# Gated attention with routed experts: the preparation as one written order per engine

## Chip, cores and metric

One core of a Trainium2 chip runs the whole program. The metric is the device time in microseconds (us) from start to end, the median of several runs.

## The reference

Four batches of 1024 tokens of width 256 pass a cross-attention on 77 context rows each, and then a mixture of 8 experts of which each token uses 2. Everything is float32.

```python
def layernorm(x, g, b):
    mu = jnp.mean(x, axis=-1, keepdims=True)
    var = jnp.mean(jnp.square(x - mu), axis=-1, keepdims=True)
    return (x - mu) * jax.lax.rsqrt(var + EPS) * g + b
...
    scores = jnp.einsum('bqe,bke->bqk', q, k) * scaling
    attn = jax.nn.softmax(scores, axis=-1)
    ctx = jnp.einsum('bqk,bke->bqe', attn, v)
    return ctx @ Wo + bo
...
    gate_logits = jnp.einsum('bsd,de->bse', x, gate_w) + gate_b
    gate_weights = jax.nn.softmax(gate_logits, axis=-1)
    topk_values, topk_indices = jax.lax.top_k(gate_weights, TOP_K)
    hidden = jax.nn.relu(jnp.einsum('bsd,edh->bseh', x, w1) + b1)
    expert_out = jnp.einsum('bseh,ehd->bsed', hidden, w2) + b2
    sel = jnp.take_along_axis(expert_out, topk_indices[..., None], axis=2)
    return jnp.sum(topk_values[..., None] * sel, axis=2)
...
x = x + jnp.tanh(g_xattn[0]) * xattn(_layernorm(x), ctx_768, ...)
x = x + jnp.tanh(g_ffn[0]) * ffn(_layernorm(x), ...)
```

## The kernel before

Each engine has its own program, written out by hand, and runs it strictly in order; semaphores are the only link. After some small folding of weights (to about 38 us) comes the **preparation** (to about 137 us), and then 71 **expert tiles** of 128 routed rows, of which attention on batches 2 and 3 is a side job.

In the preparation two works are interleaved.

*Attention of batches 0 and 1*, 8 tiles of 128 tokens each: PE turns a tile (`turn`), ACT copies it (`rows_copy`), PE computes scores against folded keys (`scores`), DVE scales them and takes the maximum (`score_in`), ACT the exponential (`softmax_exp`), PE turns (`turn_prob`), ACT copies (`prob_copy`), PE multiplies with folded values (`attend`), DVE adds to x (`residual`, after the reciprocal of `row_sums`) and takes statistics (`stats_2`, L1290). After 8 tiles follow `mean_2`, the inverse root on POOL (`root_2`, L649), the router (`choose_1`, `choose_2`, `gates`, L1316 to L1360), the place of each routed row (`position` on PE, `places` on DVE), the normalised rows (`rows_norm_2`: half on DVE; the other half on POOL for batch 0, on ACT for batch 1), their split into two float16 halves (`high_rows` on ACT, `low_rows` on DVE, L1311), and 16 indirect DMAs from POOL, which scatter them to a DRAM table sorted by expert (`scatter_rows`, L616). Rows are normalised in place, so they wait until x1, the result of attention, is stored (`store_x1` on SP; semaphore `s_outd`). SP then loads 128 sorted rows a tile.

*The experts' weights*: 8 experts, w1 (j = 0) and w2 (j = 1) each. SP loads 2 MB an expert (`load_expert`, L484). Experts 6 and 7 reuse the space of 0 and 1, so they wait for its `lo_part`s. ACT takes sums of squares (`square`, L758), PE adds them over partitions for two experts (`norms`, L1612), DVE copies them (`scales_start`), POOL takes the root (`root`, L610), DVE forms power-of-two scales (`scales`, L1003). ACT writes the float16 main part (`hi_part`, L773), DVE the float16 rest (`lo_part`, L1025). The rest of w2 of experts 2 and 7 is done by PE instead (`lo_tools`, `lo_raw`, `lo_rest`, `lo_copy`).

The order is given by loops over tiles k, with pieces of the second work put in at given k. The steps at the end of the preparation: `hidden(0)` on PE needs tile 0's rows turned (`turn_rows` on PE, L1835, `rows_T` on ACT, L922) and all w1 parts; `h_bias(0)` on ACT and `h_sum(0)` on DVE (L1516) follow `high_rows(1)` and `low_rows(1)` in their engines' orders; `hidden(1)` waits for `h_sum(0)`. A few waits:

```python
dve.wait_ge(s_pow, p + 1)              # scales(p), for root(p) of POOL
dve.wait_ge(s_ex, b + 1)               # gates(b), for gate_exp(b) of ACT
pe.wait_ge(s_m16, b + 1)               # position(b), for choose_2(b) of DVE
pe.wait_ge(s_lgc, b * T + i - 1)       # scores(b, i), for softmax_exp of tile i - 2
pe.wait_ge(s_x1, b * T + i - 1)        # attend(b, i), for residual of tile i - 2
pool.wait_ge(s_x16l, (b + 1) * T)      # first scatter of batch b, for low_rows(b)
```

## Time and profile before

| | |
|---|---|
| median of 3 runs | 586.84 us (586.26 to 587.35) |
| the profiled execution | 585.02 us |
| its span, first to last instruction | 583.3 us |
| PE busy | 512.4 us, 88% |
| ACT busy | 422.8 us, 72% |
| DVE busy | 409.0 us, 70% |
| POOL busy | 257.2 us, 44% |
| mean granted clock of PE | 0.92 of full |

The span is what the trace shows; the execution's time has 1.7 us around it. Busy shares are means over stages that differ: in the expert tiles PE is nearly always busy, in the preparation no engine is. A timeline gives start, duration, source line and operation, and in brackets the idle time before it and what ended it.

### The profile page before, as it was taken

What the parts mean: (1) busy time and instruction counts of PE and PEld (TensorE: products, weight loads), DVE (VectorE), ACT (ScalarE), POOL (GpSimd) and SP (SyncE); (2) the same over time, 40 slices, a digit from 0 to 9 for tenths busy, and PEclk for the clock granted to TensorE, in tenths of its full rate; (3) what the DMA queues carried; (4) which work ended last, traced back from release to release, by engine and by line L of the source; (5) the groups of instructions that cost most, each with busy time, mean ns of one, the idle gap of its engine ahead of it and who ended that gap; (6) DMA issues with size and microseconds to landing.
All of it is one profiled execution on the core that took longest, in us unless ns stands there. A gap on an engine that the chain in (4) does not pass through costs nothing.

```text
span 583.3 us, 15492 instructions
## 1 busy us (share of the span) xinstructions
PE 512.4 (88%) x4767; PEld 430.9 (74%) x4767; DVE 409.0 (70%) x1215; ACT 422.8 (72%) x1093; POOL 257.2 (44%) x221
## 2 busy tenths in 40 slices
PE   8968827668989999989999998999999999999991
PEld 4646415427878888778888886988999999999981
DVE  3269788898876668887666787886666666666660
ACT  1659698578656666777666766787888888888870
POOL 3110328634762225778522386875674223223222
PEclk9885565578999999999999999999999999999997
DMA  6999503145523333233433322434333232232221
GB/s 156 368 384 374 202 4 129 61 127 164 138 65 76 75 59 71 44 81 97 105 55 60 58 58 41 119 86 94 75 56 53 43 57 53 43 57 51 27 28 19
DMA packets 47969, 57.06 MB, mean 98 GB/s; under 512 B 7192, under 2 KB 43534, under 8 KB 47760
## 3 DMA queue, kind: packets, MB, share of 16 engines
q1 hardware_dynamic: 32559, 36.60, 20.7%
q0 software_dynamic: 14064, 18.55, 17.8%
q10 hardware_dynamic: 1264, 0.93, 0.5%
q8 instruction: 39, 0.64, 0.5%
q14 instruction: 43, 0.34, 0.2%
HBM read 33.19 MB, written 24.49 MB: 99 GB/s over the span
## 4 chain that ended last, share of the span: by engine, by line
PE 49%; DVE 18%; issue 10%; ACT 9%; DMA 6%; POOL 3%; SPq 3%; DVEq 1%; ACTq 1%; POOLq 0%
PE hid L1860 8%; PE hid L1864 7%; PE bank L1884 6%; PE bank L1883 6%; PE bank L1882 6%; PE hid L1863 4%; PE hid L1861 4%; ACT pool L936 3%; DVE pool L1516 3%; DMA pool<-in_L_ffn_w_dram 2%; PE bank L1843 2%; POOL xs L625 2%; PE bank L1706 2%; DVE w1l L1031 2%; DMA xs<-xext,dest 2%
## 5 line engine op out<-in xcount | busy, mean ns | idle before, releaser
L702 POOL DMA_INDIRECT out_dram<-pool,idx x71 | 114.4, 1611 | 205.4 <-DVE pool L1531 101.7
L936 ACT ACTIVATE pool<-hid,b1s 128x128 f32<-128x128 f32 x568 | 166.7, 374 | 9.6 <-PE hid L1864 2.1
L1860 PE MATMUL hid<-pool,w1h 128*128 128x256 f16 x568 | 155.5, 274 | 6.9 <-DVE pool L1516 4.9
L1882 PE MATMUL bank<-w2h,pool 128*128 x568 | 154.8, 273 | 2.2 <-issue 1.7
L1864 PE MATMUL hid<-pool,w1h 128*128 128x256 f16 x568 | 155.4, 274 | 0.0
L1883 PE MATMUL bank<-w2l,pool 128*128 x568 | 154.8, 273 | 0.0
L1884 PE MATMUL bank<-w2h,pool 128*128 x568 | 154.8, 273 | 0.0
L1516 DVE TENSOR_TENSOR pool<-hid,pool 128x512 f32<-128x512 f32 x142 | 96.0, 688 | 60.8 <-ACT pool L936 60.8
L1861 PE MATMUL hid<-pool,w1l 128*128 128x128 f16 x568 | 124.8, 220 | 0.0
L1863 PE MATMUL hid<-pool,w1l 128*128 128x128 f16 x568 | 124.8, 220 | 0.0
L945 ACT ACTIVATE pool<-pool 128x512 f16<-128x512 f32 x142 | 89.7, 636 | 41.6 <-DVE pool L1516 41.6
L1524 DVE SCALAR_TENSOR_TENSOR pool<-pool 128x512 f16<-128x512 f32 x142 | 94.5, 686 | 5.2
L625 POOL DMA_INDIRECT xs<-xext,dest x64 | 71.7, 1121 | 30.3 <-issue 17.8
L1882 PEld LDWEIGHTS bank<-w2h,pool 128*128 128x128 f16 x568 | 55.5, 98 | 10.0 <-issue 3.6
L1860 PEld LDWEIGHTS hid<-pool,w1h 128*128 x568 | 55.7, 98 | 9.6 <-issue 9.2
L1863 PEld LDWEIGHTS hid<-pool,w1l 128*128 x568 | 55.8, 98 | 6.7
L1884 PEld LDWEIGHTS bank<-w2h,pool 128*128 128x128 f16 x568 | 55.6, 98 | 6.4
L1883 PEld LDWEIGHTS bank<-w2l,pool 128*128 128x128 f16 x568 | 55.6, 98 | 6.3
L1861 PEld LDWEIGHTS hid<-pool,w1l 128*128 x568 | 55.7, 98 | 5.7
L1864 PEld LDWEIGHTS hid<-pool,w1h 128*128 x568 | 55.8, 98 | 0.0
L1531 DVE SCALAR_TENSOR_TENSOR pool<-pool,q 128x256 f32<-128x256 f32 x71 | 34.3, 483 | 21.1 <-ACT pool L952 15.7
L952 ACT ACTIVATE pool<-bank,q 128x256 f32<-128x256 f32 x71 | 33.4, 470 | 19.5 <-PE bank L1884 19.4
(276 smaller groups left out, 732.1 us busy)
## 6 DMA issues: line engine op xcount, KB each, us to landing
pool<-xs SPq DMA_DIRECT2D x71, 132.5 KB
pool<-in_L_ffn_w_dram SPq DMA_DIRECT2D x8, 1024.0 KB, 9.4
xb<-in_x_dram SPq DMA_DIRECT2D x3, 1024.0 KB, 8.6
w1h<-in_L_ffn_w_dram SPq DMA_DIRECT2D x2, 1024.0 KB, 10.8
w1l<-in_L_ffn_w_dram SPq DMA_DIRECT2D x2, 1024.0 KB, 12.0
w2h<-in_L_ffn_w_dram SPq DMA_DIRECT2D x2, 1024.0 KB, 14.1
w2l<-in_L_ffn_w_dram SPq DMA_DIRECT2D x2, 1024.0 KB, 12.4
out_dram<-xb SPq DMA_DIRECT2D x2, 1024.0 KB, 5.7
```

Source lines behind the costliest of these rows:

```text
L702: g.indirect_dma_start(out=out_rows, out_offset=bass.IndirectOffsetOnAxis(ap=idx[s % U][:, 0:1], axis=0), in_=y2[s % 3], in_offset=None, c ...
L936: a.activation(hb[:, c * P:(c + 1) * P], bank[c // 2][:, (2 * (c % 2) + 1) * P:2 * (c % 2 + 1) * P], ACT.Identity, bias=b1s[:, ds(e * NH + ...
L945: a.activation(hh[s % 2][:, half], hb[:, half], ACT.Relu).then_inc(g_hh, 1)
L1516: v.tensor_tensor(part, main, part, ALU.add).then_inc(g_hb, 1)
L1524: v.scalar_tensor_tensor(hl[s % 2][:, half], hb[:, half], 0.0, hh[s % 2][:, half], ALU.max, ALU.subtract).then_inc(g_hl, 1)
L1860: t.matmul(o, wh, xhl, start=True, stop=False)
L1861: t.matmul(o[:, 0:P], wl, xh, start=False, stop=False)
L1863: t.matmul(o[:, 0:P], wl, xh, start=False, stop=False)
L1864: mm = t.matmul(o, wh, xhl, start=False, stop=True)
L1882: t.matmul(o, hh[s % 2][:, hs], wh, start=c == 0, stop=False)
L1883: t.matmul(o, hh[s % 2][:, hs], wl, start=False, stop=False)
L1884: mm = t.matmul(o, hl[s % 2][:, hs], wh, start=False, stop=c == NH - 1)
```

## The change

The loops of the preparation are replaced by one written list of calls for ACT, DVE and PE, with another interleaving. The two semaphores of the lo_parts (`s_lo`, `s_lo1`) become one that counts all of them in the order of a list (`LOWER`), and all waits on it are restated by `lo_turn`; the hi_parts are counted by `UPPER`. `stats_1(1)` is cut in four and moved between scores; `row_sums` goes into `residual`; POOL scatters 12 rows ahead of `root(3)` instead of 13; on ACT `lo_copy(1)` comes ahead of `rows_T(0)`, and `rows_norm_2(1)` and `gate_exp(1)` behind it. `choose`, `places` and `low_rows` of batch 1 stay ahead of `h_sum(0)` on DVE. No computation is added or taken away. The diff, cut ("..." stands for lines left out; the rest of the old loops is in the listing above):

```diff
-        s_lo1 = sem("s_lo1")
...
+        UPPER = ((0, 0), (0, 1), (1, 0), (1, 1), (2, 0), (2, 1), (3, 1), (3, 0),
+                 (4, 1), (5, 0), (4, 0), (5, 1), (6, 0), (6, 1), (7, 1), (7, 0))
+        LOWER = ((0, 0), (0, 1), (1, 0), (1, 1), (2, 0), (3, 1), (3, 0),
+                 (4, 1), (5, 0), (4, 0), (6, 0), (5, 1), (7, 0), (6, 1))
+
         def hi_turn(e, j):
-            if e < E - EB:
-                return 2 * e + j + 1
-            return 2 * (E - EB) + ((1, 4), (2, 3))[e - (E - EB)][j]
+            return UPPER.index((e, j)) + 1
+
+        def lo_turn(e, j):
+            return LOWER.index((e, j)) + 1
...
-            sp.wait_ge(s_lo, 1)
+            sp.wait_ge(s_lo, max(lo_turn(0, 0), lo_turn(0, 1)))
             load_expert(6)
-            sp.wait_ge(s_lo, 2)
+            sp.wait_ge(s_lo, max(lo_turn(1, 0), lo_turn(1, 1)))
             load_expert(7)
...
-            sp.wait_ge(s_lo1, 1)
+            sp.wait_ge(s_lo, lo_turn(6, 0))
             for s in range(U):
                 load_rows(s)
-            sp.wait_ge(s_lo, E - 1)
+            sp.wait_ge(s_lo, len(LOWER))
...
-            scatter_rows(0, 0, 13)
+            scatter_rows(0, 0, 12)
             root(3)
-            scatter_rows(0, 13, KO * T)
+            scatter_rows(0, 12, KO * T)
...
-                        act.wait_ge(s_lo, e - 2)
+                        act.wait_ge(s_lo, lo_turn(e - 3, 1))
...
                 if e >= E - 2 * EB:
-                    act.wait_ge(s_lo, (3 if e < E - EB else 5) + j)
+                    act.wait_ge(s_lo, lo_turn((2 if e < E - EB else 4) + j, 0))
...
+                if b:
+                    act.wait_ge(s_lo, lo_turn(5, 1))
...
-            for k in range(T + 2):
-                if k < T:
-                    rows_copy(0, k)
-                if 1 <= k <= T:
-                    softmax_exp(0, k - 1)
-                if k >= 2:
-                    prob_copy(0, k - 2)
...
-            lo_tools(1)
-            hi_part(6, 0)
-            hi_part(7, 0)
-            hi_part(7, 1)
-            hi_part(6, 1)
-            act.wait_ge(s_nmr, 1)
-            act.wait_ge(s_outd, 2 * 16)
-            for i in range(T // 2):
-                x = xb[1][:, i, 0:D]
-                a.activation(x, x, ACT.Identity, scale=rs[1][:, i:i + 1], bias=nmr[:, i:i + 1]).then_inc(s_xn, 1)
-            gate_exp(1)
+            def rows_norm_2(b, first, last):
+                act.wait_ge(s_nmr, 1)
+                act.wait_ge(s_outd, (b + 1) * 16)
+                for i in range(first, last):
+                    x = xb[b][:, i, 0:D]
+                    a.activation(x, x, ACT.Identity, scale=rs[b][:, i:i + 1], bias=nmr[:, i:i + 1]).then_inc(s_xn, 1)
...
-            act.wait_ge(s_lo1, 1)
+            rows_copy(0, 0)
+            rows_copy(0, 1)
+            hi_part(0, 0)
+            softmax_exp(0, 0)
+            rows_copy(0, 2)
+            rows_copy(0, 3)
+            square(2, 0)
+            softmax_exp(0, 1)
+            prob_copy(0, 0)
+            softmax_exp(0, 2)
+            rows_copy(0, 4)
+            hi_part(0, 1)
+            rows_copy(0, 5)
+            prob_copy(0, 1)
+            hi_part(1, 0)
+            prob_copy(0, 2)
+            softmax_exp(0, 3)
+            softmax_exp(0, 4)
+            rows_copy(0, 6)
+            square(3, 0)
+            prob_copy(0, 3)
+            rows_copy(0, 7)
+            square(2, 1)
+            prob_copy(0, 4)
+            softmax_exp(0, 5)
+            square(3, 1)
+            prob_copy(0, 5)
+            softmax_exp(0, 6)
+            square(4, 0)
+            prob_copy(0, 6)
+            softmax_exp(0, 7)
+            hi_part(1, 1)
+            lo_tools(0)
+            prob_copy(0, 7)
+            hi_part(2, 0)
+            hi_part(2, 1)
+            square(4, 1)
+            hi_part(3, 1)
+            lo_copy(0)
+            hi_part(3, 0)
+            rows_copy(1, 0)
+            gate_exp(0)
+            square(5, 0)
+            rows_copy(1, 1)
+            rows_copy(1, 2)
+            square(5, 1)
+            square(6, 0)
+            softmax_exp(1, 0)
+            high_rows(0, 0, T)
+            prob_copy(1, 0)
+            rows_copy(1, 3)
+            square(6, 1)
+            softmax_exp(1, 1)
+            hi_part(4, 1)
+            softmax_exp(1, 2)
+            rows_copy(1, 4)
+            rows_copy(1, 5)
+            softmax_exp(1, 3)
+            prob_copy(1, 1)
+            hi_part(5, 0)
+            prob_copy(1, 2)
+            square(7, 0)
+            rows_copy(1, 6)
+            square(7, 1)
+            softmax_exp(1, 4)
+            prob_copy(1, 3)
+            hi_part(4, 0)
+            prob_copy(1, 4)
+            softmax_exp(1, 5)
+            hi_part(5, 1)
+            rows_copy(1, 7)
+            prob_copy(1, 5)
+            softmax_exp(1, 6)
+            softmax_exp(1, 7)
+            prob_copy(1, 6)
+            lo_tools(1)
+            prob_copy(1, 7)
+            hi_part(6, 0)
+            hi_part(6, 1)
+            hi_part(7, 1)
+            hi_part(7, 0)
+            lo_copy(1)
+            act.wait_ge(s_lo, lo_turn(6, 0))
             rows_T(0)
-            lo_copy(1)
+            rows_norm_2(1, 0, T // 2)
+            gate_exp(1)
             rows_T(1)
             high_rows(1, 0, T)
-            act.wait_ge(s_lo, E - 1)
+            act.wait_ge(s_lo, len(LOWER))
...
-                if (e, j) == (4, 0):
+                if j == 0 and E - 2 * EB <= e < E - EB:
-                if j == 1 or e == by_pe[0]:
-                    ins.then_inc(s_lo, 1)
-                elif e >= E - EB:
-                    ins.then_inc(s_lo1, 1)
+                ins.then_inc(s_lo, 1)
...
-            stats_1(1, 0, T)
-            mean_1(1)
...
-            def row_sums(b, first, last):
-                dve.wait_ge(s_pr, b * T + last)
-                v.reciprocal(rsum[:, first:last], psum_p[:, first:last]).then_inc(s_rsum, last - first)
-                dve.wait_ge(s_rsum, b * T + last)
-
             def residual(b, i):
-
+                dve.wait_ge(s_pr, b * T + i + 1)
+                v.reciprocal(rsum[:, i:i + 1], psum_p[:, i:i + 1]).then_inc(s_rsum, 1)
+                dve.wait_ge(s_rsum, b * T + i + 1)
                 dve.wait_ge(s_o, b * T + i + 1)
...
-            mean_2(1)
-            lo_part(6, 0)
-            dve.wait_ge(s_rs3, 2)
-            v.scalar_tensor_tensor(nmr[:], mv[1][:, :, 0], -1.0, rs[1][:], ALU.mult, ALU.mult).then_inc(s_nmr, 1)
-            choose_1(1)
-            choose_2(1)
-            rows_norm_2(1, T // 2, T)
-            lo_part(7, 0)
-            gates(1)
-            places(1)
-            lo_part(6, 1)
-            low_rows(1, 0, T)
+            def minus_mean():
+                dve.wait_ge(s_rs3, 2)
+                v.scalar_tensor_tensor(nmr[:], mv[1][:, :, 0], -1.0, rs[1][:], ALU.mult, ALU.mult).then_inc(s_nmr, 1)
...
+            stats_1(1, 0, 2)
+            score_in(0, 0)
+            stats_1(1, 2, 4)
+            score_in(0, 1)
+            stats_1(1, 4, 6)
+            score_in(0, 2)
+            lo_part(0, 0)
+            stats_1(1, 6, 8)
+            score_in(0, 3)
+            score_in(0, 4)
+            residual(0, 0)
+            lo_part(0, 1)
+            residual(0, 1)
+            stats_2(0, 0, 1)
+            score_in(0, 5)
+            mean_1(1)
+            lo_part(1, 0)
+            residual(0, 2)
+            residual(0, 3)
+            stats_2(0, 1, 2)
+            score_in(0, 6)
+            stats_2(0, 2, 3)
+            stats_2(0, 3, 4)
+            score_in(0, 7)
+            scales_start(1)
+            residual(0, 4)
+            residual(0, 5)
+            stats_2(0, 4, 5)
+            stats_2(0, 5, 6)
+            scales(1)
+            residual(0, 6)
+            lo_part(1, 1)
+            residual(0, 7)
+            stats_2(0, 6, 7)
+            stats_2(0, 7, 8)
+            mean_2(0)
+            lo_part(2, 0)
+            choose_1(0)
+            rows_norm_2(0, T // 2, T)
+            choose_2(0)
+            lo_part(3, 1)
+            lo_part(3, 0)
+            places(0)
+            gates(0)
+            score_in(1, 0)
+            scales_start(2)
+            score_in(1, 1)
+            counts_1(0)
+            scales(2)
+            low_rows(0, 0, T)
+            score_in(1, 2)
+            score_in(1, 3)
+            residual(1, 0)
+            counts_2()
+            lo_part(4, 1)
+            score_in(1, 4)
+            residual(1, 1)
+            stats_2(1, 0, 1)
+            lo_part(5, 0)
+            tables(0)
+            stats_2(1, 1, 2)
+            score_in(1, 5)
+            residual(1, 2)
+            addresses(0, FULL[0])
+            residual(1, 3)
+            lo_part(4, 0)
+            score_in(1, 6)
+            scales_start(3)
+            stats_2(1, 2, 3)
+            residual(1, 4)
+            stats_2(1, 3, 4)
+            score_in(1, 7)
+            scales(3)
+            residual(1, 5)
+            stats_2(1, 4, 5)
+            stats_2(1, 5, 6)
+            residual(1, 6)
+            residual(1, 7)
+            lo_part(6, 0)
+            stats_2(1, 6, 7)
+            stats_2(1, 7, 8)
+            lo_part(5, 1)
+            mean_2(1)
+            lo_part(7, 0)
+            minus_mean()
+            choose_1(1)
+            choose_2(1)
+            rows_norm_2(1, T // 2, T)
+            gates(1)
+            places(1)
+            lo_part(6, 1)
+            low_rows(1, 0, T)
+            dve.wait_ge(s_lo, len(LOWER))
...
-            for k in range(T + 3):
-                tile_of(0, k)
-                if k == 8:
-                    norms(1)
-            lo_raw(0)
-            lo_rest(0)
-            position(0)
...
+            turn(0, 0)
+            turn(0, 1)
+            turn(0, 2)
+            scores(0, 0)
+            turn(0, 3)
+            scores(0, 1)
+            turn_prob(0, 0)
+            scores(0, 2)
+            turn(0, 4)
+            turn(0, 5)
+            turn_prob(0, 1)
+            scores(0, 3)
+            scores(0, 4)
+            attend(0, 0)
+            turn_prob(0, 2)
+            turn(0, 6)
+            turn(0, 7)
+            attend(0, 1)
+            turn_prob(0, 3)
+            scores(0, 5)
+            scores(0, 6)
+            attend(0, 2)
+            attend(0, 3)
+            turn_prob(0, 4)
+            scores(0, 7)
+            turn_prob(0, 5)
+            attend(0, 4)
+            norms(1)
+            attend(0, 5)
+            turn_prob(0, 6)
+            attend(0, 6)
+            turn_prob(0, 7)
+            attend(0, 7)
+            lo_raw(0)
+            lo_rest(0)
+            turn(1, 0)
+            turn(1, 1)
+            position(0)
+            turn(1, 2)
+            scores(1, 0)
+            pe.wait_ge(s_ohp, 2)
+            norms(2)
+            scores(1, 1)
+            count(0)
+            scores(1, 2)
+            turn_prob(1, 0)
+            turn(1, 3)
+            attend(1, 0)
+            scores(1, 3)
+            turn(1, 4)
+            turn_prob(1, 1)
+            turn(1, 5)
+            scores(1, 4)
+            turn_prob(1, 2)
+            turn(1, 6)
+            attend(1, 1)
+            scores(1, 5)
+            turn_prob(1, 3)
+            attend(1, 2)
+            turn_table(0)
+            attend(1, 3)
+            turn_prob(1, 4)
+            scores(1, 6)
+            turn(1, 7)
+            pe.wait_ge(s_tab, 1)
+            norms(3)
+            turn_prob(1, 5)
+            attend(1, 4)
+            scores(1, 7)
+            turn_prob(1, 6)
+            attend(1, 5)
+            turn_prob(1, 7)
+            attend(1, 6)
+            attend(1, 7)
+            lo_raw(1)
+            lo_rest(1)
             pe.wait_ge(s_x1, NB * T)
             load_adr(0, 0)
             load_adr(0, 2 * NH)
             position(1)
             turn_rows(0)
             turn_rows(1)
-            pe.wait_ge(s_lo1, EB)
+            pe.wait_ge(s_lo, max(lo_turn(e, 0) for e in range(E)))
             pe.wait_ge(s_restc, 8)
             hidden(0)
             load_adr(1, 0)
             load_adr(1, 2 * NH)
             for s in range(S):
                 if s == 1:
-                    pe.wait_ge(s_lo, E - 1)
+                    pe.wait_ge(s_lo, len(LOWER))
```

## Rows read from the trace of the kernel before

**Rows 1.** Stage windows: length, busy us and count by engine, PEclk, DMA share, GB/s

```profile
100.00:120.00 20.00, 11.08 (x33) 7.38 (x34) 16.90 (x56) 11.54 (x31) 13.27 (x12) 0.50 0.17 62
400.00:500.00 100.00, 100.00 (x1096) 91.74 (x1094) 64.22 (x132) 84.04 (x222) 47.56 (x35) 1.00 0.31 56
```

**Rows 2.** Chain of waits at the first expert tile: start us, us, what

```profile
119.93 6.40 DMA xs<-xext,dest
...
134.92 1.65 DVE xext L1313
...
137.13 0.68 DVE pool L1516
```

**Rows 3.** Windows of DVE alone, cut at the end of the preparation

```profile
120.86:126.79 5.93, 5.62 (x38) 0.63 0.57 192
126.79:130.25 3.46, 3.46 (x5) 1.00 0.30 74
130.25:137.13 6.88, 6.32 (x15) 0.75 0.40 122
```

**Rows 4.** Timeline of ACT: start us, us, line, op, out<-in, count

```profile
118.93 3.88 ACT L779 ACTIVATE w1h<-pool,scl 128x2048 f16<-128x2048 f32 x2
...
126.50 2.06 ACT L905 ACTIVATE xb<-xb,nmr,rs 128x256 f32<-128x256 f32 x4
128.47 0.24 ACT L846 ACTIVATE ex<-lgd 128x64 f32<-128x64 f32 x1
```

**Rows 5.** Window of batch 0's attention

```profile
38.40:62.10 23.70, 18.41 (x63) 13.46 (x64) 20.71 (x56) 20.82 (x52) 1.64 (x1) 0.53 1.07 377
```

**Rows 6.** Timeline of SP's queue

```profile
55.20 0.37 SPq L486 DMA_DIRECT2D pool<-in_L_ffn_w_dram  x1
...
67.16 0.63 SPq L494 DMA_DIRECT2D out_dram<-xb  x1
```

**Rows 7.** Timeline of POOL, batch 0's scatters and roots

```profile
72.06 5.00 POOL L659 TENSOR_SCALAR xb<-xb,mv,rs 128x256 f32<-128x256 f32 x4 [0.89 <-DMA out_dram<-xb]
...
89.00 1.25 POOL L625 DMA_INDIRECT xs<-xext,dest  x1 [0.20 <-issue]
...
93.08 2.39 POOL L625 DMA_INDIRECT xs<-xext,dest  x1 [0.30 <-issue]
95.78 3.02 POOL L625 DMA_INDIRECT xs<-xext,dest  x1 [0.30 <-issue]
...
100.37 0.96 POOL L625 DMA_INDIRECT xs<-xext,dest  x1 [0.30 <-issue]
101.64 2.88 POOL L625 DMA_INDIRECT xs<-xext,dest  x1 [0.30 <-issue]
...
106.09 2.09 POOL L625 DMA_INDIRECT xs<-xext,dest  x1 [0.30 <-issue]
...
115.76 1.36 POOL L614 TENSOR_TENSOR nrm<-nrm,half 128x6 f32<-128x6 f32 x1 [3.79 <-DVE nrm L1001]
```

**Rows 8.** Timeline of DVE, the first lo_part beside a scatter

```profile
92.28 2.35 DVE L1031 SCALAR_TENSOR_TENSOR w1l<-w1h,scl 128x2048 f16<-128x2048 f32 x1 [1.16 <-ACT w1h L779]
```

**Rows 9.** Windows of DVE, cut to choose, gates and counts_1

```profile
71.04:74.59 3.55, 3.33 (x35) 1.00 0.13 44
74.59:75.97 1.38, 1.31 (x7) 1.00 0.00 0
97.89:99.94 2.05, 1.81 (x12) 0.50 0.18 66
```

**Rows 10.** Timeline of PE, position(1) and the first turn_rows

```profile
127.60 0.19 PE L1750 MATMUL bank<-msk,before 128*128 128x64 f16 x1 [0.87 <-DVE msk L1344]
...
129.50 0.40 PE L1843 MATMUL bank<-ident,pool 128*128 128x128 f16 x4 [1.51 <-DMA pool<-xs]
```

**Rows 11.** Windows at the first expert tile, for the clock

```profile
132.00:133.00 1.00, 0.36 (x3) 0.33 (x4) 1.00 (x3) 1.00 (x4) 0.00 (x0) 0.55 0.44 127
135.00:136.00 1.00, 1.00 (x12) 0.84 (x10) 1.00 (x1) 0.63 (x3) 0.00 (x0) 0.75 0.65 131
```

More of the change, by code:

```diff
@@ L799, in _ @@
             a.mul(cst[:], bank[6][:, 0:NC], SCALE).then_inc(s_cc, 1)
-            square(2, 0)
             def rows_copy(b, i):
@@ L1446, in attention_start @@
                     for i in tile_at(j - 4):
-                        row_sums(b, i, i + 1)
                         residual(b, i)
@@ L1532, in y_sum @@
                                        ALU.add).then_inc(g_y2, 1)
-            dve.wait_ge(s_lo, E - 1)
+            stats_1(1, 0, 2)
[12 more added lines that the diff above has]
+            stats_2(0, 0, 1)
@@ L1754, in position @@
                          start=False, stop=True).then_inc(s_pos, 1)
-            def tile_of(b, k):
-                for i in tile_at(k):
-                    turn(b, i)
-                for i in tile_at(k - 1):
-                    scores(b, i)
-                for i in tile_at(k - 2):
-                    turn_prob(b, i)
-                for i in tile_at(k - 3):
-                    attend(b, i)
-            for k in range(T + 3):
-                tile_of(0, k)
-                if k == 8:
-                    norms(1)
-            lo_raw(0)
-            lo_rest(0)
-            position(0)
-            for k in range(T + 3):
-                tile_of(1, k)
-                if k == 1:
-                    pe.wait_ge(s_ohp, 2)
-                    norms(2)
-                if k == 2:
-                    count(0)
-                if k == 6:
-                    turn_table(0)
-                if k == 8:
-                    pe.wait_ge(s_tab, 1)
-                    norms(3)
-            lo_raw(1)
-            lo_rest(1)
             def attention_mid(s):
```

87 lines of the change are left out of this document (removed).

## The prediction

> **What bounds the kernel now.** I read the stage windows first. From the first expert tile on TensorE (PE) is the bound: 100.00 busy microseconds of the hundred after 400, while between 100 and 120 it worked 11.08 of 20 at half clock and VectorE (DVE) 16.90 [rows 1]. So the preparation, up to about 137 us, is worth what it shortens, and a later start moves the end of a full PE by the same amount. The chain of waits says where the two parts meet: the last scatter of batch 0 lands (119.93 plus 6.40), then `low_rows(1)` on DVE (134.92) and `h_sum(0)` at 137.13 [rows 2]. `hidden(1)` waits for `h_sum(0)`. The change keeps `low_rows(1)` ahead of `h_sum(0)`, so I compare the start of `h_sum(0)` in both orders.
>
> DVE's windows cut the end of the preparation in three: from the end of `mean_2(1)` at 120.86 to the mask cast that ends `choose_2(1)` 5.93 us, to `gates(1)` 3.46, to `h_sum(0)` 6.88, together 16.27 [rows 3]. The after-time of `mean_2(1)` and these three stretches give the answer. I lay out the new queues with durations of the timeline of before. A score_in holds DVE 0.5 us, a residual with its reciprocal 0.6, a statistics step 0.33; a large ScalarE (ACT) operation follows its neighbour after 1.9.
>
> **Part 1, batch 0: 2.2 us gained.** `stats_1(1)` no longer stands between `scales(0)` and the first scores, `square(2, 0)` no longer ahead of the first copy. ACT now starts `hi_part(0, 0)` at 38.4, when `scales(0)` has written, and has up to `lo_tools(0)` four hi_parts (7.6), five squares (9.9), eight softmax_exp (3.4), six row copies (1.5) and seven probability copies (1.1): 23.5 us, with 0.1 to 0.2 of waits 62.1 [rows 4]. `hi_part(1, 1)` is the last of them, so `lo_part(1, 1)` runs 62.1 to 64.35. `prob_copy(0, 7)` at 62.5 gives attend at 62.8 and the last residual, behind that lo_part, ends at 64.95; two statistics steps and `mean_2(0)` make 66.5 against 68.7 before.
>
> **Part 2, a new wait of DVE: up to 3.8 us.** `load_expert(7)` waits for `lo_part(1, 1)`: 64.4 instead of 55.20 [rows 6]. Before, loads kept the DMA engines full (1.07 of their time, 377 GB/s) to about 63 [rows 5], and the store of x1 of batch 0, issued at 67.16, landed at 72.06 when GpSimd (POOL) went on [rows 7]. Now the store is issued at 65.3 right behind 2.1 MB of loads: their data run from 65.3 for 2.1 / 377 = 5.6 us to 70.9, the store's own 4.0 us (4.9 from issue to landing less 0.9 until data flow) end near 74.9. DVE reaches `rows_norm_2(0, 4..8)`, moved up to stand right behind `choose_1(0)`, at 66.5 + 2.26 (`lo_part(2, 0)`) + 2.45 = 71.2, and waits for that store. Behind it stand `choose_2(0)`, both lo_parts of expert 3, places, gates and all of batch 1. The bound below is 0, if store and loads don't queue (landed by 71). I take 3.8, because both go out on one queue. The Trainium skill, DMA: Bandwidth & Descriptors, section Queues, rings and completion order, says that each DMA engine takes the descriptors of a ring in order; by that rule too the store stands behind the loads, and no row here has a store right behind a load.
>
> From 75.0 DVE has: rows_norm 1.3, choose_2 1.15, two lo_parts 4.6, places 0.95, gates 1.38, two score_in 1.0, counts_1 2.05, scales_start and scales 1.5, low_rows(0) 2.28 [rows 3, 8, 9]: 16.2, so `low_rows(0)` ends at 91.3. PE's `position(0)`, norms(2) and count(0) and ACT's `high_rows(0)` (done 87.3) fit in. The scatters start near 91.5; before, at 89.00 behind root(2) [rows 7].
>
> **Part 3, the wait for root(3): 5.1 us.** POOL issues 12 scatters, then root(3), and `scales(3)` on DVE needs it. One scatter takes 0.96 and the next follows 1.27 after its start; but the four that met a lo_part took 2.39, 3.02, 2.88 and 2.09, that is 1.1 to 2.1 more (mean 1.6) [rows 7, 8]. Three lo_parts, (4, 1), (5, 0) and (4, 0), now fall beside the twelve: 91.5 + 15.2 + 4.9 = 111.6, and root(3), 1.36, is done at 113.3. DVE gets there earlier: from 91.3 six score_in 3.0, five residuals 3.0, three lo_parts 6.8, four statistics steps 1.3, counts_2 1.2, tables 0.85, addresses 0.6, scales_start 0.1: 16.9, thus 108.2. It waits 5.1 us. Residual(1, 5), attend(1, 7), `lo_tools(1)` and all last hi_parts stand behind. Before, this root ran at 115.76 because norms(3) was late, not the scatters. With no prolonging the wait is nil; with 2.1 each it is 6.5.
>
> The row first: all four scatters beside a lo_part were prolonged [rows 7, 8]. The Trainium skill, SBUF - State Buffer, section Who interferes with whom, says that a DVE operation with two SBUF inputs meets GpSimd's reads, not its writes, and infers that descriptor generation needs the write side. By that rule a lo_part would not hold a scatter and the sum would lose 4.9 us of POOL; this trace disagrees by 1.6 us a piece.
>
> **Part 4, to `mean_2(1)`.** From 113.3: scl after 1.1, `lo_tools(1)` 0.5, a copy 0.16, `hi_part(6, 0)` 2.0, so `lo_part(6, 0)` starts at 117.1 and ends 119.4; two statistics steps, `lo_part(5, 1)`, mean_2: 0.65 + 2.3 + 0.9. `mean_2(1)` ends at 123.25, 2.4 later than before.
>
> **Part 5, the end.** One lo_part then choose gives 5.93 again [rows 3]. But `gate_exp(1)` now stands on ACT behind `rows_T(0)` and `rows_norm_2(1)`, and `rows_T(0)` behind PE's `position(1)`, which needs the mask. From the mask's end at 126.79: position after 0.8 at 127.60, 0.4 to turn_rows (before it started only with the rows, 129.50), 0.5 to rows_T, 0.5 for it, 1.97 for the four rows (126.50 to 128.47), 0.24 for the exponential [rows 4, 10]: 4.4 until gates, where before a rows_norm and a lo_part filled 3.46. The rest is 6.88 less the 0.46 that `low_rows(1)` waited for ACT, 6.4. Sum 5.93 + 4.4 + 6.4 = 16.75; `h_sum(0)` at 123.25 + 16.75 = 140.0, or 2.9 later; adding the pieces one by one gives 140.5, so I take +3.3. `lo_copy(1)` ahead of `rows_T(0)` would give `hidden(0)` 2 us, but `hidden(1)` waits for `h_sum(0)` all the same. Tile 0's rows land near 127.5 and hold nothing. Writing `row_sums` into residual and one semaphore for two add no instruction.
>
> **The clock, 0 to 1.4 us.** PE ends `hidden(0)` near 135.8 and has nothing until 141. Before, after 5 us of small work following `lo_rest(1)`, the clock was at 0.55 in 132 to 133 and full only within 135 to 136 [rows 11]: slow for 2.7 us of work, half of it lost. I add the middle, 0.7. Total +4.0.
>
> The profiled execution took 585.02 with a span of 583.30; the three runs have a median of 586.84. So span 587.3, profiled time 589.0, median 590.8 us. A difference under 0.2% (1.2 us) can't be told from none here.
>
> **Rivals.** (1) The other side: the scatters aren't prolonged (the skill's rule above). Then root(3) is ready at 108.1, part 3 costs nothing, `mean_2(1)` ends at 118.2, `h_sum(0)` at 135.0: -2.2 + 0.7 = -1.5, 585.3 us. It decides when root(3) is done before about 110.5. The four long scatters speak against it. (2) The store holds no one: `low_rows(0)` ends 3.8 earlier, and the wait for root(3) stays, because both sides move: `h_sum(0)` at 136.2 to 136.7, time 586.6, no change. For it speaks only that no store behind a load is in the trace. (3) Both fall away: DVE never waits, about 5 us faster, 582. (4) The waits are as I say, but PE's clock falls longer and the scatters of batch 1, begun later, hold tile 9: 594 or more.
>
> **Numbers.** Forecast 0.58 (own range 588.5 to 593.5); (1) 0.18; (2) 0.12; (3) 0.08; (4) 0.04. Faster takes (3) and a little over half of (1), some 0.20; within 0.2% (2), the rest of (1) and the edge of the forecast, 0.20; slower 0.60. The range 584 to 594 leaves out (3) and the top of (4).
>
> **What the profile of the changed kernel would show.** POOL's first scatter at 91 to 92, not 89; a wait of DVE near 71 to 75 for the store; long scatters beside three lo_parts; root(3) at 112 and DVE idle ahead of it for 5 us; ACT's lo_tools(1) near 114.5; DVE idle some 3 us ahead of gates(1), released by ACT; `h_sum(0)` near 140. I am wrong if the store lands before 71, if scatters stay at 0.96 beside a lo_part, or if later tiles win back what the start loses.

## The result, and the profile after

The changed kernel takes 589.9 us (median of 5 runs, 589.46 to 592.44), the kernel before beside it 586.26 us (5 runs): a ratio of 1.0071 [1.0055, 1.0087], 0.7% slower. A second measurement on another chip gave 1.0074 [1.0056, 1.0092]. The forecast was 590.8, with 0.6 on slower. The profiled execution is the slowest of the five, 592.44 us with a span of 590.7. A second profile of the same kernel, called so below, comes from the second measurement: 590.86 us, with a span of 589.1.

The timeline of the changed kernel, DVE, at the end of batch 0's attention and up to the half of `rows_norm_2(0)`; start, duration, line, operation:

```profile
66.33 0.17 DVE L1329 TENSOR_SCALAR vv<-mv 128x8 f32<-128x8 f32 x1
66.41 2.34 DVE L1067 SCALAR_TENSOR_TENSOR w1l<-w1h,scl 128x2048 f16<-128x2048 f32 x1
70.28 0.23 DVE L1346 TENSOR_TENSOR lgd<-xb,rs 128x64 f32<-128x64 f32 x1 [1.53 <-POOL rs L656]
...
76.30 1.13 DVE L1336 TENSOR_SCALAR xb<-xb,mv,rs 128x256 f32<-128x256 f32 x3 [3.50 <-DMA out_dram<-xb]
```

`mean_2(0)` ends at 66.50, as worked out in part 1. The last line is the wait of part 2: 3.50 us for the store of x1, which SP issued at 65.31 behind `load_expert(7)`. The third line is a wait that the prediction doesn't have: `choose_1(0)` waits 1.53 us for `root_2(0)` on POOL. POOL's timeline of the changed kernel shows why, and the scatters behind it:

```profile
66.58 3.67 POOL L656 TENSOR_TENSOR rs<-vv,neghalf 128x8 f32<-128x8 f32 x1 [7.28 <-DVE vv L1329]
...
76.02 8.57 POOL L664 TENSOR_SCALAR xb<-xb,mv,rs 128x256 f32<-128x256 f32 x4 [5.62 <-DMA out_dram<-xb]
...
93.11 1.25 POOL L630 DMA_INDIRECT xs<-xext,dest  x1 [5.58 <-issue]
94.66 0.96 POOL L630 DMA_INDIRECT xs<-xext,dest  x1 [0.30 <-issue]
95.92 2.21 POOL L630 DMA_INDIRECT xs<-xext,dest  x1 [0.30 <-issue]
98.44 0.96 POOL L630 DMA_INDIRECT xs<-xext,dest  x1 [0.30 <-issue]
99.70 2.09 POOL L630 DMA_INDIRECT xs<-xext,dest  x1 [0.30 <-issue]
102.09 0.96 POOL L630 DMA_INDIRECT xs<-xext,dest  x1 [0.30 <-issue]
103.36 1.39 POOL L630 DMA_INDIRECT xs<-xext,dest  x1 [0.30 <-issue]
105.06 2.68 POOL L630 DMA_INDIRECT xs<-xext,dest  x1 [0.30 <-issue]
...
111.82 0.96 POOL L630 DMA_INDIRECT xs<-xext,dest  x1 [0.30 <-issue]
112.79 1.38 POOL L619 TENSOR_TENSOR nrm<-nrm,half 128x6 f32<-128x6 f32 x1
```

`root_2(0)`, 8 values a partition, takes 3.67 us. In the kernel before it took 1.64: there it started at 68.76 and `lo_part(2, 0)` at 68.77, now the lo_part is 0.17 ahead. `rows_norm_2(0)` on POOL took 5.00 [rows 7], now 8.57, which nothing waits for. The first scatter starts at 93.11, the twelfth ends at 112.78 and root(3) at 114.17. Four of the twelve are prolonged, together by 4.5 us; the four of before [rows 7] were by 6.5. DVE's long operations beside them, in the changed kernel:

```profile
94.96 2.35 DVE L1067 SCALAR_TENSOR_TENSOR w2l<-w1l,scl,w2h 128x2048 f16<-128x2048 f32 x1
...
98.63 2.33 DVE L1067 SCALAR_TENSOR_TENSOR w1l<-w2h,scl,w1h 128x2048 f16<-128x2048 f32 x1
...
103.31 0.60 DVE L1227 TENSOR_TENSOR VO<-prT 1x432 int32<-1x432 f32 x1
...
104.56 2.34 DVE L1067 SCALAR_TENSOR_TENSOR w1l<-w1h,scl 128x2048 f16<-128x2048 f32 x1
```

Three scatters start inside a lo_part (95.92, 99.70, 105.06) and end 0.82 to 0.84 us after it. In the kernel before it was the same: the scatter of 93.08 ended at 95.47, 0.84 after the lo_part of [rows 8]. The fourth, of 103.36, meets no lo_part but the short `addresses` (L1227, on one partition, both inputs in SBUF), and ends 0.84 after that. A scatter that is already under way isn't prolonged: those of 94.66 and 98.44 started 0.30 and 0.19 ahead of a lo_part and took 0.96. In the second profile the scatter at `addresses` took 0.96 (DVE's operation took 0.68 there instead of 0.60), the next one started 0.02 ahead of the lo_part instead of 0.50 behind, and only three scatters were prolonged, by 3.4 in all. DVE then waited 3.77 for root(3) and not 5.03.

DVE of the changed kernel at `scales(3)`, and then from `mean_2(1)` to `h_sum(0)` (L1483):

```profile
114.20 0.16 DVE L1042 SCALAR_TENSOR_TENSOR bnd<-nrm 128x2 f32<-128x2 f32 x1 [5.03 <-POOL nrm L619]
...
124.07 0.17 DVE L1329 TENSOR_SCALAR vv<-mv 128x8 f32<-128x8 f32 x1
...
128.06 0.17 DVE L1410 SCALAR_TENSOR_TENSOR nmr<-mv,rs 128x8 f32<-128x8 f32 x1 [1.57 <-POOL rs L656]
...
131.43 0.20 DVE L1372 CAST msk<-msk 128x64 f16<-128x64 f32 x1
...
135.45 0.22 DVE L1376 TENSOR_REDUCE gs<-ex 128x8 f32<-128x64 f32 x1 [2.54 <-ACT ex L852]
...
139.59 2.28 DVE L1341 TENSOR_TENSOR xext<-xb,xext 128x2048 f16<-128x2048 f32 x1
141.82 0.69 DVE L1483 TENSOR_TENSOR pool<-hid,pool 128x512 f32<-128x512 f32 x1
```

Four waits stand in it: root(3) 5.03, `root_2(1)` 1.57, the exponential 2.54, and ahead of all the store. `h_sum(0)` starts at 141.82, 4.7 us later than before [rows 2]; in the second profile at 140.90, 3.8 later. The stretches from `mean_2(1)` to the mask, to gates and to `h_sum(0)` are 7.4, 3.8 and 6.4, where [rows 3] has 5.93, 3.46 and 6.88. What ACT did ahead of the exponential (changed kernel, timeline of ACT):

```profile
132.72 0.59 ACT L879 COPY pool<-bank 128x512 f16<-128x512 f16 x1 [7.01 <-PE bank L1869]
133.20 2.08 ACT L859 ACTIVATE xb<-xb,nmr,rs 128x256 f32<-128x256 f32 x4
135.18 0.24 ACT L852 ACTIVATE ex<-lgd 128x64 f32<-128x64 f32 x1
```

From here PE pays with its clock too. Windows of the changed kernel; behind the busy times of the engines (PE, its weight loads, DVE, ACT, POOL) stand the granted clock of PE, the DMA share and GB/s:

```profile
141.00:142.00 1.00, 0.00 (x0) 0.00 (x0) 1.00 (x2) 1.00 (x5) 0.00 (x0) 1.00 0.65 262
...
144.00:145.00 1.00, 1.00 (x9) 0.82 (x8) 0.62 (x5) 0.61 (x2) 0.85 (x1) 0.50 0.38 136
...
167.00:169.00 2.00, 0.00 (x0) 0.00 (x0) 1.90 (x5) 1.36 (x3) 1.80 (x2) 1.00 0.00 1
169.00:171.00 2.00, 1.82 (x13) 1.64 (x14) 1.63 (x6) 0.76 (x3) 1.39 (x3) 0.66 0.19 68
171.00:173.00 2.00, 2.00 (x15) 1.58 (x13) 0.31 (x2) 1.30 (x5) 1.70 (x2) 0.50 0.37 136
```

After 3.3 us without work (139.3 to 142.7) `hidden(1)` runs at half clock (1.2 GHz) until 145.7, and after the pause of 167 to 169 the clock falls once more. The end of each tile on DVE (`y_sum`, L1498) dates this: tile 0 comes 5.5 us later than before, tile 3 5.6, tile 4 7.2, the last 7.4. The second profile has 5.5, 5.5, 7.1 and 5.8. So of the first shift 4.7 is `h_sum(0)` (3.8 in the second profile), and 0.8 (1.8) is left for the first fall of the clock; tile 4's step of 1.6 goes with the second fall. The kernel before has no half clock in either stretch; its own slow one is that of [rows 11].

### The profile page after: what moved, and what is told of

Its sections match the earlier page's. It is cut to its first block, busy times and chain, and to the rows that moved or that the text cites. A ratio compares the mean times of both kernels' runs of the same rounds, so it can differ in the third digit from the quotient of the medians.

```text
span 590.7 us, 15494 instructions
## 1 busy us (share of the span) xinstructions
PE 512.8 (87%) x4767; PEld 432.4 (73%) x4767; DVE 408.6 (69%) x1215; ACT 423.9 (72%) x1093; POOL 264.7 (45%) x221
## 4 chain that ended last, share of the span: by engine, by line
PE 47%; DVE 10%; issue 6%; ACT 6%; POOL 3%; DMA 2%; DVEq 1%; ACTq 1%; SPq 0%; POOLq 0%
PE hid L1886 8%; PE hid L1890 8%; PE bank L1910 6%; PE bank L1908 6%; PE bank L1909 6%; PE hid L1889 4%; PE hid L1887 4%; DVE pool L1483 3%; ACT pool L889 3%; POOL xs L630 2%; PE bank L1869 2%; PE bank L1765 2%; PE bank L1783 1%; POOL out_dram L707 1%; DVE xext L1341 1%
## 5 line engine op out<-in xcount | busy, mean ns | idle before, releaser
L1886 PE MATMUL hid<-pool,w1h 128*128 128x256 f16 x568 | 157.3, 277 | 8.5 <-DVE pool L1483 8.0
L1890 PE MATMUL hid<-pool,w1h 128*128 128x256 f16 x568 | 157.2, 277 | 0.0
L1483 DVE TENSOR_TENSOR pool<-hid,pool 128x512 f32<-128x512 f32 x142 | 96.1, 689 | 62.6 <-ACT pool L889 62.5
L630 POOL DMA_INDIRECT xs<-xext,dest x64 | 69.6, 1088 | 38.7 <-issue 22.9
L1886 PEld LDWEIGHTS hid<-pool,w1h 128*128 x568 | 56.4, 99 | 11.2 <-issue 10.8
L1889 PEld LDWEIGHTS hid<-pool,w1l 128*128 x568 | 56.5, 99 | 7.4
L1887 PEld LDWEIGHTS hid<-pool,w1l 128*128 x568 | 56.4, 99 | 6.3
L1890 PEld LDWEIGHTS hid<-pool,w1h 128*128 x568 | 56.4, 99 | 0.0
L1498 DVE SCALAR_TENSOR_TENSOR pool<-pool,q 128x256 f32<-128x256 f32 x71 | 34.3, 483 | 21.4 <-ACT pool L905 16.9
```

The costliest lines, as they stand in the source:

```text
L1483: v.tensor_tensor(part, main, part, ALU.add).then_inc(g_hb, 1)
L1886: t.matmul(o, wh, xhl, start=True, stop=False)
L1887: t.matmul(o[:, 0:P], wl, xh, start=False, stop=False)
L1889: t.matmul(o[:, 0:P], wl, xh, start=False, stop=False)
L1890: mm = t.matmul(o, wh, xhl, start=False, stop=True)
```

## The experiments

Each kernel is the changed one with the edit shown, and "the trace" is its own. Four runs and two later ones fell on chips on which every kernel, the one before too, took some 22 us more (medians of before: 608.71 and 609.14), nearly all of it in the expert tiles; there only ratios to before are compared, and times within the preparation. The other chips had before at 586.3 to 586.9.

**The store ahead of the load** (`e1_store_first`).

```diff
+            store_x1(0)
             sp.wait_ge(s_lo, max(lo_turn(1, 0), lo_turn(1, 1)))
             load_expert(7)
-            store_x1(0)
```

> The new order with one exchange on SP: store_x1(0) is issued ahead of load_expert(7). Theory (the store queued behind 2.1 MB of loads holds DVE): the store lands by about 71, DVE's idle 3.5 us ahead of rows_norm_2(0) goes, low_rows(0) and the scatters come 3.5 us earlier, the wait for root(3) stays near 5 us, h_sum(0) starts near 138.3 instead of 141.8, and the time is about 586.5, 3.5 us under the new order's. Rival (the stall was cover for the wait for root(3) behind it): that wait grows by what the store gives back, h_sum(0) stays at 141 to 142, time 590.

Ratio 1.0008 [0.9975, 1.0040]. POOL's timeline of this kernel:

```profile
71.19 4.97 POOL L664 TENSOR_SCALAR xb<-xb,mv,rs 128x256 f32<-128x256 f32 x4 [0.57 <-DMA out_dram<-xb]
...
90.03 1.25 POOL L630 DMA_INDIRECT xs<-xext,dest  x1 [5.58 <-issue]
```

The store is there at 71.2 instead of 76.0, DVE doesn't wait for it, the first scatter starts 3.1 us earlier, and `h_sum(0)` at 137.56, 4.3 earlier. Some 1 us of that isn't the edit's: the scatters fell as in the second profile, with a wait of 3.77 for root(3), and against that profile `h_sum(0)` is 3.3 earlier, about what the store had cost. By the ratio this one line is worth most of the loss of 0.7%; the interval leaves 0.3% either way.

**Root(3) behind 8 scatters, not 12** (`e2_root_after_8`).

```diff
-            scatter_rows(0, 0, 12)
+            scatter_rows(0, 0, 8)
             root(3)
-            scatter_rows(0, 12, KO * T)
+            scatter_rows(0, 8, KO * T)
```

> The new order with root(3) after 8 scatters instead of 12. Theory (DVE waits at scales(3) because POOL is still scattering): root(3) runs about 108 to 109.3, DVE's 5.0 us wait shrinks under 0.5 us. Part of it comes back: root_2(1) on POOL now stands behind eight scatters that end near 122, so choose_1(1) begins at 124.5 to 126.5 instead of 128.1, h_sum(0) 1.6 to 3.6 us earlier, time 586.3 to 588.3. Rival (something else than POOL's place in its queue sets scales(3), norms(3) for instance): DVE goes on later than 111 and the time is 589 to 590.

Ratio 1.0032 [1.0007, 1.0058]. Root(3) runs at 108.74 and DVE no longer waits for it; POOL waits 2.04 for DVE instead. But the later scatters now push `root_2(1)` back: DVE waits 3.82 for it (126.41) instead of 1.57. `h_sum(0)` 140.16. Some 2.2 us of the 5.0 were given back at the next root of the same queue. This execution is 1.1 us late from the start of the preparation on, so `h_sum(0)` gained some 2.8.

**The exponential ahead of `rows_T(0)`** (`e3_gate_exp_ahead`).

```diff
-            rows_T(0)
             rows_norm_2(1, 0, T // 2)
             gate_exp(1)
+            rows_T(0)
             rows_T(1)
```

> The new order with rows_norm_2(1) and gate_exp(1) ahead of rows_T(0) on ACT. Theory (gates(1) waits for an exponential that stands behind a copy that waits for PE): ACT, idle 7 us there, does both by 131, DVE's 2.5 us ahead of gates(1) go, h_sum(0) starts near 139.3, time about 587.4, 2.5 us less. Rival (the first tile hangs on hidden(0) or on the clock, not on DVE): no change, 589.5 to 590.

Ratio 1.0039 [1.0007, 1.0070]. The wait ahead of gates is gone and `h_sum(0)` starts at 138.32. Part of that isn't the edit's: as in the second profile, one scatter happened to start clear of a lo_part, and the wait for root(3) was 3.79. Against that profile the gain is 2.6, the 2.54 of the wait.

**The root_2 ahead of the lo_part** (`e4_root_starts_first`). DVE waits for its own last result before it issues the lo_part, in both batches:

```diff
             mean_2(0)
+            dve.wait_ge(s_vv3, 1)
+            v.memset(tick[:], 0)
             lo_part(2, 0)
...
             mean_2(1)
+            dve.wait_ge(s_vv3, 2)
+            v.memset(tick[:], 0)
             lo_part(7, 0)
```

> The new order with a wait for mean_2's last result and one tiny memset on DVE between mean_2 and the lo_part behind it, twice, so that POOL's root_2 starts some 0.1 us before the lo_part. Theory (root_2 takes 3.7 us instead of 1.65 because the lo_part started first and holds it off): both root_2 take about 1.65, choose_1(1) starts about 1.4 us earlier, h_sum(0) near 140.4, time about 588.5; what choose_1(0) wins is lost again to the store's wait. Rival (the 3.7 us have another cause, or a started root is held off as well): root_2 stays at 3.7 and the time is 0.2 us up.

Ratio 1.0055 [1.0022, 1.0088]; against 1.0071 the time alone settles nothing. The timeline does. POOL, then DVE:

```profile
66.39 1.64 POOL L656 TENSOR_TENSOR rs<-vv,neghalf 128x8 f32<-128x8 f32 x1 [7.27 <-DVE vv L1329]
...
66.35 2.38 DVE L1067 SCALAR_TENSOR_TENSOR w1l<-w1h,scl 128x2048 f16<-128x2048 f32 x1
```

1.64 instead of 3.67, in batch 1 1.67 instead of 3.70, and the waits of 1.5 are gone. In batch 0 the gain went into the next wait: that for the store grew from 3.50 to 4.83. `h_sum(0)` starts at 140.2, 1.6 earlier.

**What holds a scatter.** Two kernels give the three lo_parts beside the twelve scatters, (4, 1), (5, 0) and (4, 0), another form, for the timing alone: what they write is no longer the rest of the weights. First a multiplication without the subtraction, with one input in SBUF instead of two (`e5_one_input`):

```diff
+                if (e, j) in ((4, 1), (5, 0), (4, 0)):
+                    ins = v.tensor_scalar(wl[:, ds(e * n, n)], src, scl[:, e, j:j + 1], rs[0][:, 0:1], ALU.mult, ALU.mult)
+                else:
```

> The new order, in which the three lo_parts that fall beside batch 0's scatters, (4, 1), (5, 0) and (4, 0), are written as one multiplication of the raw weights by their scale, without subtracting the main part: same size, one operand in SBUF instead of two (it leaves out the subtraction, for the timing). Theory (a DVE operation holds POOL because of its second SBUF operand): no scatter beside them is prolonged, the twelve end near 108.3 instead of 112.8, root(3) is done near 109.7 and DVE's wait at scales(3) falls from 5.0 to about 1 us. Rival (any long DVE operation holds a scatter's descriptors): scatters stay at 2 to 2.7 us and the wait at 4 to 5.

One run, 589.84 us. DVE's and POOL's timelines of this kernel:

```profile
96.37 1.34 DVE L1068 TENSOR_SCALAR w2l<-w1l,scl,rs 128x2048 f16<-128x2048 f32 x1
...
99.03 1.33 DVE L1068 TENSOR_SCALAR w1l<-w2h,scl,rs 128x2048 f16<-128x2048 f32 x1
...
96.07 1.76 POOL L630 DMA_INDIRECT xs<-xext,dest  x1 [0.30 <-issue]
98.14 0.96 POOL L630 DMA_INDIRECT xs<-xext,dest  x1 [0.31 <-issue]
99.40 1.80 POOL L630 DMA_INDIRECT xs<-xext,dest  x1 [0.30 <-issue]
```

Three scatters are still prolonged, by 0.8 to 0.9 each. Those of 99.40 and 105.30 start inside the operation and end 0.84 after it, as beside a lo_part; but that of 96.07 was 0.30 under way, which a lo_part lets pass, and ended 0.12 after the operation. The operation also changed its rate, 1.34 us instead of 2.34, so that this run doesn't separate operands and rate. The next form is a reduction over axes of length one: one input, as many elements, 2.28 us, its output left unscaled (`e9_reduce`, `e10_reduce_again`).

```diff
+                if (e, j) in ((4, 1), (5, 0), (4, 0)):
+                    ins = v.tensor_reduce(wl[:, ds(e * n, n)], src.rearrange("p (a b) -> p a b", b=1), AX.X, ALU.max)
+                else:
```

> The changed kernel with the three lo_parts (4, 1), (5, 0) and (4, 0) replaced by a tensor_reduce over axes of length one: one SBUF operand, the same 2048 elements a partition read and written, and, unlike the tensor_scalar of the one-operand run, no form that should run at twice the rate. Their output is left unscaled, so it isn't the rest of the weights; nothing later depends on it in time. If every DVE operation of this kind holds a scatter, whatever its operands, the operation takes 2.1 to 2.4 us and scatters that start inside it take 2.0 to 3.0 us, and DVE waits some 5 us for root(3) as before. If only a second SBUF operand or the faster form holds them, these scatters take 0.96 and the wait for root(3) falls to about 2 us or less. The first has 7 in 10: the one-operand run stretched scatters to 1.8 us, but there the faster form could have been the cause.

Eleven of the twelve scatters took 0.96 to 1.01 (the first 1.25, as in [rows 7]), so the likelier expectation, 7 in 10, was wrong. `h_sum(0)` came no earlier all the same: DVE stood 2.76 ahead of a residual and 1.98 ahead of score_in(1, 7), with no releaser in this kernel that the trace shows. So the kernel was run once more, and timed:

> The kernel of the reduce run once more, now timed. In its first profile the twelve scatters ran at 0.96 us beside 2.28 us reduces and root(3) was done at 112.2 with no wait of DVE for it, but DVE stood still ahead of a residual (2.8 us) and ahead of score_in(1, 7) (2.0 us) with no releaser in the trace, and h_sum(0) came no earlier. If that standstill was an accident of one execution on a chip with slower transfers, it is gone here, the start of h_sum(0) falls by 4 to 5 us against the changed kernel, to 136 to 137.5, and the ratio comes to 0.998 to 1.001. If it belongs to this order of work (something else that holds all engines once the scatters run closer together), it is there again and the ratio stays near 1.006.

Ratio 0.9995 [0.9978, 1.0013]. The standstill isn't there. DVE, then POOL, of this second run:

```profile
98.23 2.27 DVE L1068 TENSOR_REDUCE w1l<-w2h 128x2048 f16<-128x2048 f32 x1
104.11 2.28 DVE L1068 TENSOR_REDUCE w1l<-w1h 128x2048 f16<-128x2048 f32 x1
...
98.12 0.96 POOL L630 DMA_INDIRECT xs<-xext,dest  x1 [0.30 <-issue]
99.38 0.96 POOL L630 DMA_INDIRECT xs<-xext,dest  x1 [0.30 <-issue]
...
108.11 1.37 POOL L619 TENSOR_TENSOR nrm<-nrm,half 128x6 f32<-128x6 f32 x1
```

Root(3) is done at 109.48, DVE waits 0.86 for it, `h_sum(0)` starts at 137.15: 3.75 earlier than in the second profile of the changed kernel. What the standstill of the first run was stays open.

One other reading is left, that a scalar_tensor_tensor holds a scatter whatever its inputs. The changed kernel's own trace speaks against it: `residual` (L1315) is the same operation with one input in SBUF and one in PSUM. DVE, then POOL:

```profile
107.88 0.49 DVE L1315 SCALAR_TENSOR_TENSOR xb<-bank,rsum,xb 128x264 f32<-128x264 f32 x1
...
108.04 0.96 POOL L630 DMA_INDIRECT xs<-xext,dest  x1 [0.30 <-issue]
```

The scatter starts 0.16 inside and takes 0.96; an end 0.83 after the operation would have made it 1.16.

**All four edits together** (`e6_all`: the store first, 8 scatters, the exponential ahead, both memsets of e4), beside the changed kernel itself on the same chip (`after_again`).

> The new order unchanged, beside the others on their chip, as their yardstick: ratio to the kernel before 1.007, as in the first measurement.

> The new order with all four edits: store ahead of the last load, root(3) after 8 scatters, gate_exp ahead of rows_T, root_2 started first. Theory (four separate waits on one chain): scatters start near 89.5, root(3) is done by 106.5, but root_2(1) stands behind the last eight scatters and runs near 121.5, so choose_1(1) starts near 123 instead of 128 and h_sum(0) near 134.5, 7.4 us earlier than in the new order; ratio to the kernel before about 0.995. Rival (they hide each other): no more than the best of them alone, ratio 1.000 or above.

The changed kernel 1.0074 [1.0056, 1.0092]; with the four edits 0.9907 [0.9887, 0.9927], `h_sum(0)` at 133.20. One large wait is left, DVE:

```profile
122.05 0.18 DVE L1410 SCALAR_TENSOR_TENSOR nmr<-mv,rs 128x8 f32<-128x8 f32 x1 [3.82 <-POOL rs L656]
```

**`root_2(1)` between the scatters** (`e7_root2_between`: the four edits, and POOL's order `scatter_rows(0, 8, 13)`, `root_2(1)`, `scatter_rows(0, 13, KO * T)`).

> As the run before, and root_2(1) moved between the 13th and the 14th scatter of batch 0. Theory (root_2(1) behind the scatters is the last of POOL's waits): it runs as soon as mean_2(1) is done, near 116, choose_1(1) starts near 117.5, and h_sum(0) is then set by tile 0's rows and hidden(0), near 130.5; 11 us earlier than in the new order, ratio to the kernel before about 0.989. Rival (tile 0's rows, whose last three scatters now come later, take its place at once): h_sum(0) at 134 or later, ratio 0.995 as without the move.

0.9887 [0.9862, 0.9911], 578.57 us against 586.44: faster than both kernels. `h_sum(0)` starts at 131.35, 1.85 before that of the four edits; the times of the two aren't told apart (0.9887 and 0.9907, intervals that overlap). DVE's last large wait is this:

```profile
129.14 2.29 DVE L1342 TENSOR_TENSOR xext<-xb,xext 128x2048 f16<-128x2048 f32 x1 [3.88 <-ACT xext L834]
```

**`high_rows(1)` ahead of `rows_T(0)`** as well (`e8_high_rows_ahead`, and once more on another chip as `e11_high_rows_again`).

```diff
             gate_exp(1)
+            high_rows(1, 0, T)
             rows_T(0)
             rows_T(1)
-            high_rows(1, 0, T)
```

> The best version so far (ratio 0.989) with high_rows(1) on ACT moved from behind rows_T(1) to right behind gate_exp(1). The theory: DVE's last large wait, 3.9 us ahead of low_rows(1), is only for high_rows(1), which stood behind rows_T(0) and so behind tile 0's rows. Then the wait goes, h_sum(0) comes near 128.5 instead of 131.4, hidden(0) begins up to 2 us later but hidden(1) waits for h_sum(0) all the same: 2 to 3 us off, ratio 0.984 to 0.986. The rival: rows_T(0), 1.9 us later, delays hidden(0), h_bias(0) and with them h_sum(0), so that the bound moves from DVE to PE and ACT: a gain of under 1 us, ratio 0.988 or above.

0.9854 [0.9815, 0.9893], on one of the chips where every kernel takes longer in the tiles, with `h_sum(0)` at 131.95 behind ACT. The interval holds both expectations, therefore:

> The kernel with high_rows(1) ahead of rows_T(0) once more, on another chip than its first time, where tile 0's rows came late and h_sum(0) waited 2.6 us for h_bias(0) on ACT. The theory (DVE's 3.9 us wait was the bound): h_sum(0) near 128.5, ratio 0.984 to 0.986. The rival (hidden(0), h_bias(0) and h_sum(0) now hang on the rows of tile 0, so little is left to gain over 0.989): h_sum(0) at 130.5 or later behind ACT, ratio 0.987 to 0.990.

0.9885 [0.9849, 0.9921]. This interval, too, reaches to the theory's range; the trace decides for the rival, though with `h_sum(0)` at 130.20 and not 130.5 or later. DVE and ACT of this run:

```profile
130.20 0.69 DVE L1484 TENSOR_TENSOR pool<-hid,pool 128x512 f32<-128x512 f32 x1 [2.55 <-ACT pool L890]
...
121.74 1.90 ACT L834 CAST xext<-xb 128x2048 f16<-128x2048 f32 x1 [2.38 <-DMA xs<-xext,dest]
```

DVE's wait is gone and stands ahead of `h_sum(0)` instead: `hidden(0)` and `h_bias(0)` hang on tile 0's rows, and `high_rows(1)` on the landing of batch 0's last scatter. The move gave 1.15 us at `h_sum(0)` and nothing in the time that can be told. By these waits the scatters and tile 0's rows behind them are the bound now; no run tried that.

## Why the prediction was right, step by step

**The bound.** That PE passes a shift of `h_sum(0)` on held in every profile from the faster chips: 4.7, 3.8, 4.1, 0.0, -3.9, -5.8 and -6.9 us at `h_sum(0)` (the two profiles of the changed kernel, e5, e10, e6, e7, e11) went with 7.4, 5.8, 4.8, 3.2, -3.7, -7.6 and -6.4 at the last tile. The up to 3.2 us beside it are put down to the clock and to the spread of single executions.

**Part 1** was right: 66.5. What the step didn't see is that the better start put `lo_part(2, 0)` ahead of `root_2(0)`. The wait of 1.53 that came of it hid in front of the store's in batch 0 (e4), but 1.57 counted in full in batch 1.

**Part 2** was right in its cause: with the store ahead of the load, e1, the wait is nil. That its size came out, 3.50 for 3.8 predicted, is in part luck. The store was there at 76.0 to 76.3 and not at 74.9, and DVE came to it at 72.8 and not at 71.2, because it had lost 1.53 to `root_2(0)`; in e4, without that loss, it waited 4.83. Rival 2 said 586.6, no change, for that case; e1 measured 1.0008.

**Part 3** was right in its cause, and in size once: 5.03 for 5.1 in the one profile, 3.77 in the other. It put 4.9 on three scatters beside a lo_part, at a mean of 1.6. They cost 4.1, and `addresses`, which it didn't have, 0.4; in the second profile all together cost 3.4. The mean isn't a price: a held scatter ends some 0.83 after the operation in which it starts, so that beside a lo_part it costs from 0.4 (e7) to 2.1 us [rows 7] by where it falls, and nothing if it starts just ahead. The first scatter started at 93.11, not 91.5: `low_rows(0)` ended 0.7 later than worked out, and the scatter starts 1.1 after its end. DVE came 1.0 later as well, so the difference stayed.

Rival 1, scatters that aren't prolonged, described e10 rightly and was 1.2 us too fast: it said 585.3, and e10's 0.9995 is 586.5 on the prediction's 586.84. `h_sum(0)` started at 137.15 and not at 135.0; missing were again the wait for `root_2(1)`, 1.57, and a rest of 0.86 at root(3).

Part 3 went by the rows and set a rule against them, by which a lo_part wouldn't hold a scatter. The rows were right, and the rule, read to its end, agrees with them. The Trainium skill, SBUF - State Buffer, section Who interferes with whom, counts among DVE's operations that meet GpSimd those with two SBUF inputs and those in a two-port mode, which a tensor_scalar can take, and says that a tensor_reduce never meets it on trn2. The three forms here agree: 2.34 us with two inputs prolongs a scatter that starts inside it to as much as 3.0, 1.34 us with one input prolongs it to 1.8, and the reduction of 2.28 us leaves it at 0.96. By the same section of the Trainium skill two inputs meet only what reads SBUF, and it infers that they spare the generation of descriptors. The traces don't refute that inference: a scatter reads its row numbers (`dest`) from SBUF, and one already under way, by 0.02 to 0.30 us, passes a lo_part at 0.96, while the tensor_scalar of e5 held one that was 0.30 under way. That what a lo_part holds is this read fits both, and wasn't tried.

**Part 4** said 123.25, measured 124.24: root(3) 0.9 later.

**Part 5** was half right. The wait for the exponential is there, 2.54, and e3 removes it; from the mask's end to gates it is 3.8, not 4.4, since position starts 0.05 behind the mask and not 0.8. The 0.8 of [rows 10] were taken for latency; that they were the register loads which stand ahead of position(1) in PE's program is a guess, and wasn't tried. The missing 1.57 for `root_2(1)` and the 1.0 of part 4 outweigh the 0.6 that gates came sooner: 141.82 against 140.0 to 140.5.

**The clock** was put at 0.7, for one fall after 5 us in which PE has nothing, from 135.8 on. What is left for that fall at tile 0 is 0.8 (1.8 in the second profile). But `hidden(0)`, itself at half clock until 138.5, ended only at 139.3, and the pause was 3.3 us (3.8): the first number came out though its working did not. The step of 1.65, 1.64 and 1.65 us at tile 4, in both profiles of the changed kernel and in e10, was missed; nothing of it is there in e6, e7 and e11. PE pauses 2.4 to 2.7 us ahead of tile 4 in all of these and in the kernel before, whose clock stays full. What makes it fall there isn't shown. It doesn't simply follow from the first fall: e5 and e4 have half clock at `hidden(1)` (142 to 148, 140 to 146) and none behind it up to 200, while e3 and e8 have none at `hidden(1)` and then have it at 167 to 171 and 172 to 176.

The total: +4.0 was forecast, and +3.6 was measured between the medians. The cause, a bound at `h_sum(0)` that is pushed back by the store, by held scatters and by the exponential, was right. That the number is so close is in part luck: predicted were 3.3 at `h_sum(0)` and 0.7 behind it, while the second profile, of an execution near its median (590.86 against 590.46), has 3.8 and 2.0, together 5.8 over the profile of before. That one was of an execution 1.8 us under its median (585.02 against 586.84), and so was the base of the sum. What an ordinary execution of the kernel before loses there is on no trace.

## What to carry to other kernels

In a queue that is written out by hand, look at what stands behind each moved instruction on the slowest shared queue: a store behind a load of 2 MB cost 3.5 us, and swapping the two lines gave it back. When a root is needed by another engine, give it its own place between long runs of other work, and follow where the gain goes: moving root(3) alone gave 2.2 of 5 us to the next root. The four edits together turned 0.7% slower into 0.9% faster, and with the second root moved it is 1.1%, a step that shows at `h_sum(0)` and not in the time. A wait that is cleared ahead of the bound shows in the trace long before it shows in the time, so judge single edits by the trace and the sum by the time. And take a second profile of the same kernel before a difference of 1 us is given to an edit: two profiles of the changed kernel differ by 0.9 us at `h_sum(0)`, by the place of one scatter.
